# Neighbour sums: rows as three bf16 parts in place of two 4-byte halves

## The reference, cut to what matters

```python
def _L1_gnn_ref(feat, W_self, W_neigh, src, dst):
    h_self = feat @ W_self
    h_neigh = feat @ W_neigh
    h_sparse = _maxk(h_neigh, MAXK)          # the 32 largest of 256 in each row, the rest 0
    msg = h_sparse[src]
    summed = jax.ops.segment_sum(msg, dst, num_segments=n)
    deg = jax.ops.segment_sum(jnp.ones((src.shape[0],), dtype=feat.dtype), dst, num_segments=n)
    neigh = summed / jnp.maximum(deg, 1.0)[:, None]
    return h_self + neigh
    ...
    x = x + _L1_gnn_ref(_layernorm(x, axis=-1), L1_gnn_W_self, L1_gnn_W_neigh, src, dst)
```

## Time and profile before

| | us |
|---|---|
| time, median of 3 runs (4351.14 to 4359.82) | 4351.2 |
| span of the profiled execution, first to last instruction | 4349.6 |
| of it sparse_table, about 3015 to 3196 | 181 |
| of it neighbour_sums, about 3196 to 3951 | 755 |
| before sparse_table; after neighbour_sums | 3015; 399 |
| PE busy in the whole span | 3703.0 |

### The profile page before, as it was taken

How to read it: one execution, slowest core, us unless ns; L and a number is a source line. 1 busy time by engine, 2 the same in 40 slices (tenths; PEclk the granted TensorE clock), 3 DMA queues, 4 the chain that set the end, 5 groups by cost and what they waited for, 6 DMA issues and landing times. The chain is left out here.

```text
span 4349.6 us, 73406 instructions
## 1 busy us (share of the span) xinstructions
PE 3703.0 (85%) x19616; PEld 2744.7 (63%) x19641; DVE 2690.5 (62%) x9486; ACT 1684.8 (39%) x3943; POOL 2823.1 (65%) x2869
## 2 busy tenths in 40 slices
PE   4999996778777778877699999978769999996988
PEld 2566663444445556746588888866348888884657
DVE  8766656656544443445555455557978888886862
ACT  3444453434323333323344444446523333333320
POOL 5777777777777777772577777751667767672230
PEclk9999997776689999975799999999879999997998
DMA  7555553333434443531423323336379999993001
GB/s 252 188 193 186 188 191 119 105 105 105 115 115 124 125 123 106 164 105 43 91 66 69 69 66 70 70 101 213 117 279 385 368 367 385 373 385 95 1 1 59
DMA packets 354620, 682.83 MB, mean 157 GB/s; under 512 B 69218, under 2 KB 181104, under 8 KB 347853
## 3 DMA queue, kind: packets, MB, share of 16 engines
q0 software_dynamic: 133184, 338.60, 25.7%
q1 hardware_dynamic: 221039, 339.52, 23.1%
HBM read 565.53 MB, written 112.35 MB: 156 GB/s over the span
## 5 line engine op out<-in xcount | busy, mean ns | idle before, releaser
L1070 POOL DMA_INDIRECT e_ring<-table,erow x1040 | 1004.6, 966 | 316.9 <-issue 165.2
L1488 PE MATMUL e_sums<-e_ring,e_onehot 128*128 128x257 f32 x2080 | 821.2, 501 | 297.4 <-DMA e_ring<-table,erow 250.4
L2587 POOL DMA_INDIRECT t_source<-source_rows,t_index x632 | 606.9, 960 | 209.0 <-issue 157.2
L1488 PEld LDWEIGHTS e_sums<-e_ring,e_onehot 128*128 128x128 f32 x2080 | 379.7, 226 | 564.5 <-issue 332.6
L1600 POOL DMA_INDIRECT e_ring<-table,esrc x544 | 531.1, 976 | 212.9 <-issue 128.3
L560 POOL DMA_INDIRECT r_ring<-rows,esrc x400 | 449.7, 1124 | 149.7 <-issue 93.0
L1036 ACT ACTIVATE k_sign<-ramp,low 128x128 bf16<-128x128 f32 x1024 | 364.1, 395 | 447.9 <-PE e_sums L1459 429.7
L1685 PE MATMUL e_total<-e_loads,e_times 128*128 128x256 f32 x3072 | 502.7, 300 | 17.2 <-DMA e_loads<-table 12.3
L1685 PEld LDWEIGHTS e_total<-e_loads,e_times 128*128 128x128 f32 x3072 | 409.3, 190 | 69.5 <-issue 35.2
L1583 ACT ACTIVATE e_times<-e_tally 128x320 fp32r<-128x320 f32 (+4 forms) x640 | 259.7, 426 | 484.8 <-PE e_tally L1669 480.0
L2771 PE MATMUL t_raw<-big,t_w 128*128 128x256 f32 x1600 | 377.9, 390 | 20.2 <-ACT t_hidden L2606 19.4
(11 more groups left out here) (560 smaller groups left out, 6336.4 us busy)
## 6 DMA issues: line engine op xcount, KB each, us to landing
e_loads<-table SPq DMA_DIRECT2D x512, 256.0 KB
table<-r_stage SPq DMA_DIRECT2D x49, 1024.0 KB
outputs<-first_outputs SPq DMA_DIRECT2D x49, 512.0 KB, 6.6
first_outputs<-t_stage SPq DMA_DIRECT2D x96, 256.0 KB
t_near<-near_rows SPq DMA_DIRECT2D x79, 256.0 KB
e_ring<-table,erow POOLq DMA_INDIRECT x1040
table<-n_split SPq DMA_DIRECT2D x49, 256.0 KB
t_source<-source_rows,t_index POOLq DMA_INDIRECT x632
```

The costliest lines, as they stand in the source:

```text
L1070: eng.indirect_dma_start(ring[:, t % RING, 0:D], None, table, bass.IndirectOffsetOnAxis(ap=b.erow[:, EARLY + t:EARLY + t + 1], axis=0)).th ...
L1488: eng.matmul(sums[g % SUMS][:, 0:ACCW], onehot[t % ONEHOTS][:, :], ring[:, t % RING, :], start=(t % GROUP == 0), stop=(t % GROUP == GROUP ...
L2587: eng.indirect_dma_start(source[s][:, q, :], None, a.source_rows, bass.IndirectOffsetOnAxis(ap=index[s][:, q:q + 1], axis=0)).then_inc(gat ...
```

## The change

The rows of table3 become three bf16 parts of 512 bytes each (1.5 KB a row): the value rounded to bf16, the rest of it rounded to bf16, and the rest of that. One-hot matrices, counts and loaded rows are bf16 too, and there are three matmuls where there were two. The ring gets 16 slots in place of 12. In sparse_table ACT makes the first two parts (head, middle), POOL the two subtractions (remain, last), and DVE no part of it any more. The self part is no longer added by POOL: PE adds the features themselves into the left half of the product, by a product with the identity, and ACT copies that half back to the features (semaphore kept), and the right half to n_full in a second instruction.

```diff
-UPPER = -(1 << 12)
+THIRDS = 3
...
-    RING = 12
+    RING = 16
...
-        ring = sb("e2_ring", [P, RING, 2, D], F32R)
-        onehot = [sb(f"e2_onehot{s}", [P, P], F32R) for s in range(ONEHOTS)]
+        ring = sb("e2_ring", [P, RING, THIRDS, D], BF16)
+        onehot = [sb(f"e2_onehot{s}", [P, P], BF16) for s in range(ONEHOTS)]
...
-        times = [sb(f"e2_times{s}", [P, DWIDE * P], F32R) for s in range(TIMES)]
-        loads = sb("e2_loads", [P, AHEAD, 2, D], F32R)
+        times = [sb(f"e2_times{s}", [P, DWIDE * P], BF16) for s in range(TIMES)]
+        loads = sb("e2_loads", [P, AHEAD, THIRDS, D], BF16)
...
-                eng.indirect_dma_start(ring[:, t % RING, :, :].rearrange("p n d -> p (n d)").bitcast(F32), None, halves, bass.IndirectOffsetOnAxis(
+                eng.indirect_dma_start(ring[:, t % RING, :, :].rearrange("p n d -> p (n d)"), None, thirds, bass.IndirectOffsetOnAxis(
...
-                eng.tensor_scalar(onehot[t % ONEHOTS][:, :], b.ramp[:, 0:P], b.edst[:, FROM + t:FROM + t + 1], None,
+                eng.tensor_scalar(onehot[t % ONEHOTS][:, :], rampr[:, :], b.edst[:, FROM + t:FROM + t + 1], None,
...
-                    for half in range(2):
+                    for third in range(THIRDS):
                         mm = eng.matmul(part(n, q), times[g % TIMES][:, q * P:(q + 1) * P],
-                                        loads[:, g % AHEAD, half, :], start=False, stop=False, skip_group_check=True)
+                                        loads[:, g % AHEAD, third, :], start=False, stop=False, skip_group_check=True)
                 mm.then_inc(spread, 1)
...
-                for half in range(2):
-                    mm = eng.matmul(sums[g8 % 2][:, 0:D], onehot[t % ONEHOTS][:, :], ring[:, s, half, :],
-                                    start=(half == 0 and t % GROUP == 0), stop=(half == 1 and t % GROUP == GROUP - 1))
+                for third in range(THIRDS):
+                    mm = eng.matmul(sums[g8 % 2][:, 0:D], onehot[t % ONEHOTS][:, :], ring[:, s, third, :],
+                                    start=(third == 0 and t % GROUP == 0),
+                                    stop=(third == THIRDS - 1 and t % GROUP == GROUP - 1))
                 mm.then_inc(summed, 1)
...
-        full = [sb(f"n_full{s}", [P, 2, D]) for s in range(WAYS)]
+        full = [sb(f"n_full{s}", [P, D]) for s in range(WAYS)]
...
         sparse = [sb(f"n_sparse{s}", [P, D]) for s in range(WAYS)]
-        split = [sb(f"n_split{s}", [P, 2, D]) for s in range(WAYS)]
+        parts = [sb(f"n_parts{s}", [P, THIRDS, D], BF16) for s in range(WAYS)]
+        rest = [sb(f"n_rest{s}", [P, D]) for s in range(WAYS // 2)]
...
             def choose(w):
                 eng.wait_ge(masked, w + 1)
+                wait_if(eng, first, w - WAYS + 1)
                 wait_if(eng, stored[w % WAYS], 32 * (w // WAYS))
-                eng.tensor_tensor(sparse[w % WAYS][:, :], mask[w % WAYS][:, :], full[w % WAYS][:, 1, :], ALU.mult).then_inc(chosen, 1)
-
-            def part(w):
-                eng.wait_ge(headed, w + 1)
-                eng.tensor_tensor(split[w % WAYS][:, 1, :], sparse[w % WAYS][:, :], split[w % WAYS][:, 0, :],
-                                  ALU.subtract).then_inc(parted, 1)
+                eng.tensor_tensor(sparse[w % WAYS][:, :], mask[w % WAYS][:, :], full[w % WAYS][:, :], ALU.mult).then_inc(chosen, 1)
+
+            def remain(w):
+                eng.wait_ge(first, w + 1)
+                wait_if(eng, third, w - len(rest) + 1)
+                eng.tensor_tensor(rest[w % len(rest)][:, :], sparse[w % WAYS][:, :], parts[w % WAYS][:, 0, :],
+                                  ALU.subtract).then_inc(rested, 1)
+
+            def last(w):
+                eng.wait_ge(second, w + 1)
+                eng.tensor_tensor(parts[w % WAYS][:, 2, :], rest[w % len(rest)][:, :], parts[w % WAYS][:, 1, :],
+                                  ALU.subtract).then_inc(third, 1)
...
-            for w in range(NW):
-                eng.wait_ge(evacuated, w + 1)
-                eng.tensor_tensor(b.x[:, w, :], b.x[:, w, :], full[w % WAYS][:, 0, :], ALU.add).then_inc(added, 1)
-                if w >= LATER:
-                    choose(w - LATER)
-                if w >= LATER + BEHIND:
-                    part(w - LATER - BEHIND)
-            for w in range(NW - LATER, NW):
-                choose(w)
-                part(w - BEHIND)
-            for w in range(NW - BEHIND, NW):
-                part(w)
...
+            for w in range(NW + 2):
+                if w < NW:
+                    choose(w)
+                if 1 <= w <= NW:
+                    remain(w - 1)
+                if w >= 2:
+                    last(w - 2)
+            eng.wait_ge(third, NW)
...
-            def head(w):
-                eng.wait_ge(chosen, w + 1)
-                wait_if(eng, stored[w % WAYS], 32 * (w // WAYS))
-                eng.tensor_tensor(split[w % WAYS][:, 0, :].bitcast(I32), sparse[w % WAYS][:, :].bitcast(I32),
-                                  upper[:, 0:D].bitcast(I32), ALU.bitwise_and).then_inc(headed, 1)
...
-                if not isinstance(i, int) or i > 0:
-                    for w in range(WAYS * i - GROUP4, WAYS * i):
-                        head(w)
                 search(here(GROUP4))
-                for w in range(WAYS * i, WAYS * i + GROUP4):
-                    head(w)
...
+                wait_if(eng, kept, w - 1)
                 for k in range(KH):
                     mm = eng.matmul(product[s][:, :], xt[s][:, k, :],
                                     weights[:, k, :, :].rearrange("p n d -> p (n d)"),
                                     start=(k == 0), stop=(k == KH - 1))
+                    if k == 0:
+                        eng.matmul(product[s][:, 0:D], b.ident[:, :], b.x[:, w, :], start=False, stop=False)
                 mm.then_inc(multiplied, 1)
...
+            def head(w):
+                eng.wait_ge(chosen, w + 1)
+                wait_if(eng, stored[w % WAYS], 32 * (w // WAYS))
+                eng.activation(parts[w % WAYS][:, 0, :], sparse[w % WAYS][:, :], ACT.Copy).then_inc(first, 1)
+
+            def middle(w):
+                eng.wait_ge(rested, w + 1)
+                eng.activation(parts[w % WAYS][:, 1, :], rest[w % len(rest)][:, :], ACT.Copy).then_inc(second, 1)
+
+            def split(w):
+                if w >= 0 and w < NW:
+                    hide(w)
+                if w - 1 >= 0 and w - 1 < NW:
+                    head(w - 1)
+                if w - 2 >= 0 and w - 2 < NW:
+                    middle(w - 2)
...
                     norm(w + 2)
                 if w + 1 < NW:
                     copy(w + 1)
-                if w >= LATER:
-                    hide(w - LATER)
+                split(w - LATER)
                 eng.wait_ge(multiplied, w + 1)
                 wait_if(eng, chosen, w - WAYS + 1)
-                wait_if(eng, added, w - WAYS + 1)
-                eng.activation(full[w % WAYS][:, :, :].rearrange("p n d -> p (n d)"), product[w % 2][:, :],
-                               ACT.Copy).then_inc(evacuated, 1)
-            for w in range(NW - LATER, NW):
-                hide(w)
+                eng.activation(b.x[:, w, :], product[w % 2][:, 0:D], ACT.Copy).then_inc(kept, 1)
+                eng.activation(full[w % WAYS][:, :], product[w % 2][:, D:2 * D], ACT.Copy).then_inc(evacuated, 1)
+            for w in range(NW - LATER, NW + 2):
+                split(w)
+            eng.wait_ge(kept, NW)
```

More of the change, by code:

```diff
@@ L1491, in _, with neighbour_sums @@
                     tally(t)
-def neighbour_sums(nc, b, table, halves):
+def neighbour_sums(nc, b, table, thirds):
     ONEHOTS = BODY
-    RING = 12
+    RING = 16
     MARKS = 8
@@ L1571, in _ @@
                 wait_if(eng, spread, g - AHEAD + 1)
-                eng.dma_start(loads[:, g % AHEAD, :, :].rearrange("p n d -> p (n d)").bitcast(F32),
-                              halves[bass.ds(low, P), :]).then_inc(fetched[g % AHEAD], 16)
+                eng.dma_start(loads[:, g % AHEAD, :, :].rearrange("p n d -> p (n d)"),
+                              thirds[bass.ds(low, P), :]).then_inc(fetched[g % AHEAD], 16)
             for s in range(AHEAD):
@@ L3047, in sparse_table @@
         product = [ctx.enter_context(nc.psum_tensor(f"n_product{s}", [P, BANK], F32)) for s in range(2)]
-        upper = ctx.enter_context(nc.psum_tensor("n_upper", [P, BANK], F32))
-        bounded = sem("n_bounded")
         loaded = sem("n_loaded")
@@ L3062, in sparse_table @@
         chosen = sem("n_chosen")
-        added = sem("n_added")
+        kept = sem("n_kept")
         cleared = sem("n_cleared")
         stored = [sem(f"n_stored{s}") for s in range(WAYS)]
-        headed = sem("n_headed")
-        parted = sem("n_parted")
+        first = sem("n_first")
+        rested = sem("n_rested")
+        second = sem("n_second")
+        third = sem("n_third")
         block = ctx.enter_context(nc.Block())
```

(30 more changed lines are left out.)

## The result

The changed kernel takes 4460.3 us (median of 4 runs, 4456.2 to 4465.2) against 4351.2 (4349.0 to 4359.8): a ratio of 1.0247, 95% interval 1.0235 to 1.026. It is slower by 109 us; 124 was forecast, in a range of +91 to +204.

A forecast was written before the change was run, and what follows sets the result against it. The prediction took PE to pace neighbour_sums, transfers close behind, and DVE to be full in sparse_table. 181 - 9 - 30 - 6 = +136 us there and -12 in sparse_table made +124, 4475 us from 4351.2, range 4442 to 4555.

The forecast's parts named there:

- 109 ns a matmul: neighbour_sums on PE: a 2-byte matmul of 256 columns comes every 109 ns, against 120 with 4-byte operands; bounds 107 and 120.
- Rival 1: neighbour_sums: a bf16 matmul also comes only every 120 ns, from the change of weights; +193, 4544 us; chance 0.11.
- a count straight after 4-byte matmuls is slower: neighbour_sums on PE: two 2-byte counts of 256 columns were read as 0.12 us from first to second.
- Rival 3: neighbour_sums: 2-byte rows stream faster, 120 ns being a limit of bytes; at half of 120, -182, 4169 us; chance 0.03.
- +181 us for the third matmul at the smaller price: neighbour_sums on PE: 4160 matmuls at 120 ns (499 us) become 6240 at 109 ns (680 us); bounds +169 and +250.
- -9 for changes of type: neighbour_sums on PE: switching between 2-byte counts and 4-byte sums, 128 times, costs nothing afterwards; -9 us.
- -30 for late loads: neighbour_sums: PE's waits for late loads go, with three quarters of the bytes and a slower PE; -30 us, bounds 0 and -47.
- -6 at the end: End of neighbour_sums: PE's 6.2 us of waits for gathered rows go, as 16 slots hold the last 16 ahead; -6 us.
- -12 us in sparse_table: sparse_table: DVE loses its heads, -19 us, against +3, +2 and +2 of losses; -12 us, bounds -18 and +5.
- +7 us of losses: sparse_table: identity product at the start +3, longer chain at the end +2, late starts in some groups +2.
- The share of the transfers near 0.65: neighbour_sums: the transfers' share falls from 1.02 to near 0.65, their rate from 377 to about 240 GB/s.
- Nothing for DVE, POOL and ACT under a longer stage: neighbour_sums: one-hots, copies and gathers change little, and these engines (617, 522, 260 us busy) have room; 0 us.

The follow-up runs named there:

- wide rows: The changed kernel with rows of 2 KB again (a fourth part of zeros, stored and fetched but not multiplied) and a ring of 12 slots: 4463.6 us.
- the run with two of three parts: The changed kernel with its third matmul taken away, the third part of every neighbour's row left out of the sums; table and transfers stay: 4284.9 us.

## Why the prediction was right, and where its steps were not

- **That neighbour_sums is paced by PE, and 109 ns a matmul**: right. The 109 was read off four counts of 320 columns and came out to the nanosecond, with fp16 as with bf16. Rival 1 (120 ns) rested on the pair of 256 columns, and so did the prediction's sentence that a count straight after 4-byte matmuls is slower. That was a misreading. The pair at 3595.19 and the four sums behind it last until the next sums begin:

```profile
3595.89 0.40 PE L1697 MATMUL e_sums<-e_ring,e_onehot 128*128 128x256 f32 x2
```

  That is 0.70 us, which is 2 x 0.109 + 4 x 0.120, so pair and sums together took no more than their parts, and the 0.12 us between two record starts is no price of the pair. Rival 3 (2-byte rows stream faster) falls with the 109 ns of the changed kernel.
- **+181 us for the third matmul at the smaller price, -9 for changes of type**: right. The steps of the table give 250 of work less 76 for the type.
- **-30 for late loads and -6 at the end**: the term was too small, and its cause only half right. 181 - 9 - 123 = 49 us went, against 36. I put them down to three quarters of the bytes; but three 4-byte matmuls with full rows lose 48 us of waits as well, and wide rows bring none of them back. Smaller rows end the late loads (-36 in the kernel before), and a slower PE ends them too. The change does both, so the one is worth nothing where the other is. So the term came near for a reason that was only half of it, which was luck: smaller rows without the third matmul were good for 36 us, and in the changed kernel they are good for none.
- **-12 us in sparse_table**: right in sum (-13.2), by errors that cancel, so by luck. The heads were taken as twelve times 1.6 us, from the start that the next search could have had; 1.26 us a group went (13.16 between two searches against 11.90), eleven times between the first and the last replacement, where 13.7 us went (159.4 to 145.7) rather than 19. Of the +7 us of losses 3 came: the start with the identity grew by 1.6 in place of 3, the chain at the end by 1.3 in place of 2, and late starts cost nothing in place of 2. And 2.3 us were gained from the last part to the first sum (11.4 to 9.0), for which the prediction has nothing; what gained them the runs don't show. That DVE would hardly wait for ACT's longer chain was right. Its waits for copies in the changed kernel all lie in the first 15 us of the stage:

```profile
DVE n_best L3141 <- ACT n_full L3254: 13.2, 4, 7.4
```

- **The share of the transfers near 0.65**: wrong, it is 0.80 at 242 GB/s. I scaled it by bytes. The share falls more slowly than the bytes do.
- **Nothing for DVE, POOL and ACT under a longer stage**: right; DVE is busy 613 us in this stage, as against 617 before, POOL 516 against 522 and ACT 259 against 260. **The clock** held at 0.99.

## What to carry to other kernels

Where TensorE is the full engine, the cost of an operand's format is first the number of matmuls it needs and then the nanoseconds of each: a type of half the size bought 11 ns in 120 and asked for half as many matmuls again. A wait that two resources share goes away when either of them gets slack, so price the relief of the second one with the slowdown of the first already in place. And price an operation that is taken away by the distance between two like operations around it, not by the earliest start that the gap would allow.

## What the runs showed of the hardware

- A matmul of 256 columns with two 4-byte (F32R) operands comes every 120 ns, with bf16 or fp16 every 109, each with a weight load of its own; 107 are its columns (at 2.4 GHz, the granted clock being 0.98 to 0.99). A pair of 128-column bf16 counts between 4-byte sums costs 0.07 us more than its parts; a pair of 256 columns costs nothing more (0.70 us with four sums, 3595.19 to 3595.89).
- The transfers' busy share and their rate don't go together: 377 GB/s at a share of 1.02 with 2 KB in two pieces of 4-byte values (the kernel before), 319 at 0.92 with 2 KB rows of bf16, 242 at 0.80 with 1.5 KB, 201 at 0.70 with 1 KB. Per unit of share that is 370, 347, 302 and 287 GB/s. It isn't the row alone: the run with two of three parts has 1.5 KB too, and 326. With the same rows and ring its busy time is 0.92 x 694.5 = 639 us, that of the changed kernel 0.80 x 861.9 = 690, so the busy time grows with the time of the stage too. Why isn't settled; a share scaled down by bytes comes out too low either way.
- A gather of 128 rows by POOL comes round every 1.27 to 1.28 us where POOL hardly pauses, with rows of 1 KB and of 1.5 KB alike.
